# Walking the second FFN product chunk by chunk in more groups, with eight output slots and a split last tile

## The reference

```python
x = x + xattn(layernorm(x), ctx, Wq, Wk, Wv, Wo, bo)
xq   = act_fake_quant(layernorm(x), clip_x)
gate = xq @ weight_fake_quant(w_gate).T
up   = xq @ weight_fake_quant(w_up).T
h    = act_fake_quant(silu(gate) * up, clip_down)     # scale: one maximum over all of |h|
x    = x + h @ weight_fake_quant(w_down).T
```

## Time and profile before

| | |
|---|---|
| median of 3 runs | 555.96 us |
| the profiled execution | 555.49 us |
| its span (first to last instruction) | 553.7 us |
| granted TensorE clock, mean over the span | 0.994 of full speed |
| PE busy | 532.5 us, 96% |
| DVE busy | 473.2 us, 85% |
| ACT busy | 294.8 us, 53% |
| POOL busy | 231.6 us, 42% |

### The profile page before, as it was taken

How to read it: one execution, slowest core, us unless ns; L and a number is a source line. 1 busy time by engine, 2 the same in 40 slices (tenths; PEclk the granted TensorE clock), 3 DMA queues, 4 the chain that set the end, 5 groups by cost and what they waited for, 6 DMA issues and landing times.

```text
span 553.7 us, 7998 instructions
## 1 busy us (share of the span) xinstructions
PE 532.5 (96%) x2685; PEld 357.4 (65%) x2693; DVE 473.2 (85%) x874; ACT 294.8 (53%) x414; POOL 231.6 (42%) x349
## 2 busy tenths in 40 slices
PE   8989889999999999999997999999999999899997
PEld 7878678887888888787876644444444446343443
DVE  4967888989989898998988599999999988879783
ACT  4743646556465655544535445545545534999200
POOL 4386759689595867856443000000000000154441
PEclk9999999999999999999999899999999999999999
DMA  8718365856657574625788736842244020399887
GB/s 314 267 58 300 110 176 176 267 152 216 209 189 237 189 251 134 192 77 203 162 218 280 189 74 250 322 115 41 75 114 113 17 62 1 150 327 208 112 110 119
DMA packets 82514, 93.82 MB, mean 169 GB/s; under 512 B 46785, under 2 KB 49601, under 8 KB 82217
## 3 DMA queue, kind: packets, MB, share of 16 engines
q1 hardware_dynamic: 77449, 84.13, 48.5%
q0 software_dynamic: 4320, 7.87, 9.6%
q10 hardware_dynamic: 704, 1.31, 0.8%
HBM read 47.51 MB, written 37.78 MB: 154 GB/s over the span
## 4 chain that ended last, share of the span: by engine, by line
PE 46%; issue 35%; DVE 12%; DMA 4%; ACT 1%; POOL 1%; SPq 0%; DVEq 0%; POOLq 0%
PE QO L193 5%; PE QO L195 5%; PE QO L194 5%; PE SP L464 5%; DMA out<-n2b 2%; PE PTP L1238 2%; PE MI L584 2%; PE MI L582 2%; PE MI L583 2%; PE QO L1238 2%; PE SP L1238 2%; PE PTP L517 2%; DVE bn L614 1%; DVE xTs L224 1%; DMA ctr<-in_ctxT 1%
## 5 line engine op out<-in xcount | busy, mean ns | idle before, releaser
L45 POOL DMA_DIRECT2D out<-n2b x30 | 30.2, 1039 | 215.3 <-DVE n2b L1249 215.3
L1139 ACT ACTIVATE sil<-QO,fsc 128x512 f32<-128x512 f32 x88 | 60.5, 687 | 72.3 <-PE QO L1133 72.3
L1133 PE MATMUL QO<-nT,wgu 128*128 128x512 bf16 x352 | 90.3, 379 | 0.6 <-ACT nT L220 0.6
L1133 PE MATMUL SP<-nT,wgu 128*128 128x512 bf16 x352 | 90.3, 379 | 0.0
L1143 DVE SCALAR_TENSOR_TENSOR h<-SP,fsc,sil 128x512 f32<-128x512 f32 x88 | 65.9, 749 | 9.9 <-PE SP L1133 9.9
L505 POOL TENSOR_TENSOR PN<-P,rs 128x512 f32<-128x512 f32 x64 | 44.2, 713 | 50.3 <-DVE rs L497 50.3
L1146 DVE TENSOR_REDUCE hmx<-h 128x1 f32<-128x512 f32 x88 | 60.4, 686 | 3.0
L1133 PEld LDWEIGHTS QO<-nT,wgu 128*128 128x128 bf16 x352 | 34.4, 98 | 42.0 <-ACT nT L220 0.7
L1133 PEld LDWEIGHTS SP<-nT,wgu 128*128 128x128 bf16 x352 | 34.5, 98 | 41.5
L488 ACT ACTIVATE P<-P,r 128x616 f32<-128x616 f32 x32 | 26.0, 811 | 63.5 <-DVE P L484 63.5
L193 PE MATMUL QO<-xTs,wqs 128*128 128x512 f32 x124 | 50.4, 406 | 2.3 <-DVE xTs L224 2.0
(11 more groups left out here) (200 smaller groups left out, 1191.0 us busy)
## 6 DMA issues: line engine op xcount, KB each, us to landing
xTr<-in_xT SPq DMA_DIRECT2D x8, 1024.0 KB, 7.7
xn<-in_x SPq DMA_DIRECT2D x32, 256.0 KB, 3.8
out<-x SPq DMA_DIRECT2D x32, 256.0 KB, 2.9
n_rows<-n SPq DMA_DIRECT2D x32, 256.0 KB, 2.6
n2b<-n_rows SPq DMA_DIRECT2D x32, 256.0 KB, 3.7
out<-n2b POOLq DMA_DIRECT2D x30, 256.0 KB, 4.4
h_spill<-h SPq DMA_DIRECT2D x2, 2816.0 KB, 9.9
h<-h_spill SPq DMA_DIRECT2D x6, 768.0 KB, 7.7
```

The source lines that it names most:

```text
L1133: m = e.matmul(ps, wv_[:, k, col:col + 128], nT[:, b % 2, :, k, :], start=(k == 0), stop=(k == 3))
L1139: t_sil[n] = add("act", lambda e: e.activation(sil[:, n % SR, :], gp, ACT.Silu, scale=fsc[:, ic:ic + 1]), [t_g[n], t_fs, t_h.get(n - SR)] ...
```

## The change

- Groups 0, 1 and 2 go chunk by chunk over their four tiles (`PART_MAJOR = 3`, `down_parts`); groups 3 to 7 go tile by tile as before.
- In groups 1 and 2, the quantizing of the next group's chunks 0 to 2 stands ahead of all four output steps in VectorE's list, and chunk 3, with the clips still open, ahead of the third. The second clip of the last chunk of group 0 and of all chunks of group 1 follows its first clip at once.
- The output slots are eight in place of six. The rows of tiles 30 and 31 are loaded into two slots of `sil`, the buffer of the first product's activations, once the last block of h is made.
- Tile 31 is multiplied in two halves of 256 columns, in banks 7 and 3, each with its own eleven matmuls, its own two VectorE steps and its own transfer.

```diff
-            t_xl1[m] = dma("sp", xo[:, 6 + m - LAST[0], :], out_v[n], [t_x1s[n], t_q1[31]], f"ld_x1b{m}")
+            t_xl1[m] = dma("sp", sil[:, m - LAST[0], :], out_v[n], [t_x1s[n], t_h[NB * NI - 1]], f"ld_x1b{m}")
...
             finish_h()
             halfway.append((i, p, qv, a))
+            if (i, p) == (0, NI - 1) or i == 1:
+                finish_h()
...
+        def down_last(tt):
+            at = {}
+            for half, ps in ((0, down_bank[7]), (1, down_bank[3])):
+                w = slice(256 * half, 256 * half + 256)
+                def fn(e, ps=ps, w=w):
+                    for k in range(NI):
+                        mm = e.matmul(ps[:, w], hq[:, (NB - 1) % 2, k, tt * 128:tt * 128 + 128], wd[:, k, w],
+                                      start=(k == 0), stop=(k == NI - 1))
+                    return mm
+                t = add("pe", fn, [done[NB - 1, 3], t_om[23], t_om[27]], "dn_mm")
+                at[half] = ps[:, w], w, t
+            return at
...
-            so = m % 6
+            so = m % 8
+            if m == 31:
+                for half, (view, w, t) in down_last(tt).items():
+                    a = add("dve", lambda e, view=view, w=w: e.tensor_tensor(xo[:, so, w], view, sdb[:, w], ALU.mult),
+                            [t, t_sds, t_os[m - 8]], "o_m")
+                    a = add("dve", lambda e, w=w: e.tensor_tensor(xo[:, so, w], xo[:, so, w], sil[:, 1, w], ALU.add),
+                            [a, t_xl1[m]], "o_a")
+                    t_os[m] = dma("sp", out_v[n][:, w], xo[:, so, w], [a], "st_p1")
+                return
...
-                          [t_dn[m], t_sds, t_os.get(m - 6), t_q1[31]], "o_m")
+                          [t_dn[m], t_sds, t_os.get(m - 8), t_q1[31]], "o_m")
...
+        PART_MAJOR = 3
+
+        def down_parts(i):
+            for p in range(len(parts_of[i])):
+                for tt in range(4):
+                    down_part(i, tt, p)
+
+        down_parts(0)
         quant_h(1, 1)
         for i in range(NB):
+            if 0 < i < PART_MAJOR:
+                down_parts(i)
+            if 0 < i < PART_MAJOR:
+                for p in range(3):
+                    quant_h(i + 1, p)
             for tt in range(4):
-                if i + 1 < NB and (i > 0 or tt < 2):
-                    quant_h(i + 1, tt if i else tt + 2)
-                    if (i, tt) == (0, 1) or (i > 0 and tt == 3):
+                if i == 0 and tt < 2:
+                    quant_h(1, tt + 2)
+                if 0 < i < PART_MAJOR and tt == 2:
+                    quant_h(i + 1, 3)
+                    finish_h()
+                if PART_MAJOR <= i < NB - 1:
+                    quant_h(i + 1, tt)
+                    if tt == 3:
                         finish_h()
-                if i > 0:
+                if i >= PART_MAJOR and (i, tt) != (NB - 1, 3):
                     for p in range(4):
                         down_part(i, tt, p)
                 down_out(i, tt)
```

More of the change, by code:

```diff
@@ L1246, in down_out @@
             ps = down_bank[m % 8]
-            t_dn[m] = ("dn_mm", c.count["dn_mm"]) if i else t_dn[m]
-            so = m % 6
+            so = m % 8
[7 more added lines that the diff above has]
+                return
             t_om[m] = add("dve", lambda e: e.tensor_tensor(xo[:, so, :], ps, sdb[:, :], ALU.mult),
-                          [t_dn[m], t_sds, t_os.get(m - 6), t_q1[31]], "o_m")
+                          [t_dn[m], t_sds, t_os.get(m - 8), t_q1[31]], "o_m")
             if m in LAST:
-                t_oa[m] = add("dve", lambda e: e.tensor_tensor(xo[:, so, :], xo[:, so, :], xo[:, 6 + m - LAST[0], :],
+                t_oa[m] = add("dve", lambda e: e.tensor_tensor(xo[:, so, :], xo[:, so, :], sil[:, 0, :],
                                                                ALU.add), [t_om[m], t_xl1[m]], "o_a")
-                t_os[m] = dma("sp", out_v[n], xo[:, so, :], [t_oa[m]], f"st_p{m % 6}")
+                t_os[m] = dma("sp", out_v[n], xo[:, so, :], [t_oa[m]], "st_p0")
             else:
-                t_os[m] = c.dma_add(out_v[n], xo[:, so, :], [t_om[m], t_x1s[n]], f"st_o{m % 6}")
+                t_os[m] = c.dma_add(out_v[n], xo[:, so, :], [t_om[m], t_x1s[n]], f"st_o{m % 8}")
         for i in range(NB):
@@ L1266, in block_kernel @@
         quant_h(1, 0)
-        for p in range(NI):
-            for tt in range(4):
-                down_part(0, tt, p)
+        PART_MAJOR = 3
[4 more added lines that the diff above has]
+        down_parts(0)
         quant_h(1, 1)
         for i in range(NB):
-            for tt in range(4):
-                if i + 1 < NB and (i > 0 or tt < 2):
-                    quant_h(i + 1, tt if i else tt + 2)
-                    if (i, tt) == (0, 1) or (i > 0 and tt == 3):
+            if 0 < i < PART_MAJOR:
[3 more added lines that the diff above has]
+                    quant_h(i + 1, p)
+            for tt in range(4):
+                if i == 0 and tt < 2:
[6 more added lines that the diff above has]
+                    if tt == 3:
                         finish_h()
-                if i > 0:
+                if i >= PART_MAJOR and (i, tt) != (NB - 1, 3):
                     for p in range(4):
```

## The result

The changed kernel took 551.02 us in the median of six runs (549.97 to 553.25), the kernel before 555.9 (555.16 to 556.65) beside it: a ratio of 0.9916, interval 0.9897 to 0.9936, that is 4.9 us less. In a later measurement eight runs gave 551.56 against 555.56 of the kernel before, ratio 0.9927 (0.9903 to 0.9950), 4.0 less. The forecast was 552.0, 3.9 less, in a range of 551.0 to 553.6. The two measurements differ by 0.9 us in what the change is worth. Their intervals overlap, so that difference is not clear of noise; where it may come from is the first question of the experiments.

What follows compares the result with a forecast made beforehand. TensorE bounds the second FFN product, stalling for VectorE's quantized chunks, before a VectorE and DMA tail. 3.23 + 0.51 + 0.2 = 3.94 us off 555.96 gives 552.0 us; own range 551.0 to 552.8, range with rivals 551.0 to 553.6.

Steps and rivals of the forecast that it cites:

- the sum: Whole gain: 3.23 us from chunk order, 0.51 and 0.2 from the tail, 0 for slots; 3.94 us less.
- The size of the stalls: Second FFN product: TensorE loses 3.29 us waiting for quantized chunks, 1.99 without group 3's 1.30.
- The forecast's own sign: Trace after, second FFN product: TensorE's waits for quantized chunks under 0.3 us in all.
- Part 1, the walk: VectorE's new order in groups 1 to 3: chunks come in time, taking 3.23 us off.
- a charge of 0.06: Group 3's chunk 2 comes level with TensorE's want; 0.06 us booked as lost there.
- Part 2, cost and worth of the slots: Eight output slots and moved loads and reloads in SP's queue: cost put at 0.
- Part 3, the tail: Last tile in halves: matmuls cost nothing extra, last issue 0.51 us sooner, last transfer 0.2 less.
- The stall did not move to group 3: Rival: TensorE stalls at group 3's first tile, up to 1.30; gain 2.7, 553.3 us; chance 0.14.
- the tail gave its gain: Rival: half transfers eat 0.7, 552.7 us, or exposed weight loads cost 1.06, 553.1; chance together 0.14.
- no slot came late: Rival: late landings make output 12 block VectorE and group 4 starve; 558.0 us if 8 late; chance 0.08, slower 0.03.
- the stage before 468 would not move: Sign: the forecast is wrong if the first product's stage, before 468 us, moves at all.

Runs made afterwards that it cites:

- clips_slots_only: The changed kernel with groups 1 and 2 tile by tile; early clips, eight slots and halves stay: 553.25 us, ratio 0.9944.
- six_slots: The changed kernel with six output slots in place of eight: 553.77 us, ratio 0.9958.
- late_clip: The changed kernel with the immediate second clips of groups 0 and 1 taken out again: 551.06 us in one run.
- after_again: The changed kernel, unchanged, measured again later: 551.56 us.
- warm_before: The kernel before with twelve more warming matmuls (results unread) ahead of the first scale: 554.71 us, ratio 0.9989.
- warm_after: The changed kernel with twelve more warming matmuls (results unread) ahead of the first scale: 549.98 us, ratio 0.9901.

## Why the prediction was right, and where it was not

The time was 551.0 and 551.6 in two measurements, the forecast 552.0. In the stage, where the change acts, the gain was 4.3 us against 3.9 in the sum. The prediction was right in the size of the stalls and in the walk, and partly by luck in what it gave the gain to. By its own steps:

- *The size of the stalls* (3.29 us). Right in place, 0.2 too small. The matmul at 470.23, from which group 0 was counted, is the second of the pair in QO (tiles 0 and 1); the pair in SP (tiles 2 and 3) begins at 470.45, so the first lay two paces before that, at 470.02, its record missing. Group 0 was through at 479.52, and the stall at group 1's start is 0.27, not 0.06: 3.50 in all. After, 0.08 is left: 3.42 gained on TensorE against 3.23 in the sum. (The forecast's own sign, chunk waits under 0.3 us in the view, was missed: the view shows 0.4, of which the matmuls lost 0.08.)
- *Part 1, the walk.* Every chunk came in time where the walk said so, and the one place without margin, group 3's third chunk, lost 0.08 against a charge of 0.06. But the sum booked all of it on the chunk order. The runs split it: chunk order 1.6 (clips_slots_only), eight slots 0.9 (six_slots), early clips 0.3 (late_clip, one run), each against the changed kernel; the 0.6 missing to 3.4 goes only with more than one of them. Group 3's 1.30, which the sum gave to the chunk order, was gone without it in clips_slots_only.
- *Part 2, cost and worth of the slots.* This step failed. It asked whether eight slots would hold anything up, found no wait and wrote 0; it did not ask what the six had cost. VectorE's waits for output transfers in the old trace, 2.3 us in the view that was read and 4.0 by the landings, stand ahead of group 3's clips: with six slots TensorE loses 1.02 at group 3 even when groups 1 and 2 go chunk by chunk. With six slots the loss also follows the landings (stage 87.4 in one trace, 88.0 in the other, with 4.0 and 4.6 us of slot waits); with eight it is 83.1 in all three. That the forecast came out all the same was luck: its sum took all of group 3's loss as gained, whichever part gained it.
- *Part 3, the tail.* The half-width matmuls cost 0.109, as taken; the issue came 0.5 sooner after the last column, as walked. The transfer of a half lands in 1.7 and the span ends 2.2 after its issue, against 2.5: about 0.3 where 0.2 was taken. The rule in the Trainium skill's "TensorE: Matmul & The Clock Gate" (The mechanism), that weight loads hide only behind other row groups, is contradicted again: 98 ns loads at a pace of 109.
- *The rivals.* The stall did not move to group 3, the tail gave its gain, and in the profiled run no slot came late: output 4 landed 1.7 before its slot was wanted. The margin is thin, though. In the second execution (after_again) output 3 took 15.1 us to land and VectorE stood 0.17 for its slot, with the same stage of 83.1. The forecast also read output 4's old landing 0.5 too late: it was issued at 486.84 and landed at 500.9, not 501.4.
- *The clock.* The forecast said the stage before 468 would not move. It did, by 1.2 us between the two profiled runs, and by 3.3 between two executions of the changed kernel alone, so this sign could not tell right from wrong. The length of the half-clock stretch at the first scale gives 1.2 and 1.3 of these. It may also be behind the 0.9 us between the two measured gains; that was not shown, and it limits what any forecast could be held to here.

## What to carry to other kernels

When an edit bundles an order, a buffer count and an early step, price each by what it removes from the old trace, not by whether it causes a wait in the new one; the waits of an engine that is not the bound count if what stands behind them in its list feeds the bound. Walk the list of the feeding engine in its order, with start-to-start times for independent steps and full durations for dependent ones. Where executions of one kernel differ by as much as the edit, measure a stage between two fixed instructions in the traces, and check that it is the same in two traces of the same kernel. Where a wait is put down to an engine that had long been done, look up when the transfer that also stands in the wait landed: here one wait of 1.1 to 1.6 us in each of three traces with six slots belonged to a slot.

## What the runs showed of the hardware that was not expected

- The clock's fall at the first scale costs time in a kernel in which TensorE is 97% busy: from the first scale's transpose to the first FFN matmul it is 7.9 us or 9.1 to 9.2 in the traces of the kernels before and after, with the clock at 0.50 there for a shorter or a longer stretch, and 6.4 and 6.7 in warm_before and warm_after, with the clock at 1.00.
- Matmuls that keep the clock up can themselves be the wait: ten of them behind the second scale held the first product back by 0.7 us once its chunk came early.
- On VectorE a step that works on the result of the one before starts 1.00 us after it (475.50, 476.50 in the changed kernel), one that doesn't 0.87 (476.74, 477.61 in the earlier trace rows), behind the same first step of 0.96 us.
- A 256 KB transfer that adds to DRAM took 3.8 us from issue to landing late in the kernel before and up to 14.1 beside SP's reloads; the wait for a slot depends on it.
